# Edges ranked in 80 half-target buckets, one 314-column count matmul per chunk

## The reference

```python
for r in range(weight.shape[0]):
    mask = (edge_type == r).astype(x.dtype)
    sums = jax.ops.segment_sum(msgs * mask[:, None], dst, num_segments=n)
    cnt = jax.ops.segment_sum(mask, dst, num_segments=n)
    mean = sums / jnp.maximum(cnt, 1.0)[:, None]
    out = out + mean @ weight[r]
```

## Time and profile before

| what | us |
|---|---|
| median of three runs | 1880.85 |
| span of the profiled execution, first to last instruction | 1878.8 |
| what lies around the span, taken as median less span | 2.05 |
| edge tables, 38.2 to 142.0 | 103.8 |
| scatter, 142.0 to 242.3 | 100.3 |
| histogram, 242.3 to 429.0 | 186.7 |
| all that follows | 1449.8 |

### The profile page before, as it was taken

The page is one execution under the profiler, slowest core; times in us unless marked ns, Lnnn a source line. Parts: engine busy times, 40 slices in busy tenths (PEclk is TensorE's granted clock), DMA queues, the critical chain, the costliest instruction groups (busy, mean ns, idle before and its releaser), DMA issues.

```text
span 1878.8 us, 28666 instructions
## 1 busy us (share of the span) xinstructions
PE 1794.9 (96%) x9953; PEld 1477.4 (79%) x9953; DVE 1023.3 (54%) x2540; ACT 478.5 (25%) x1055; POOL 701.1 (37%) x609
## 2 busy tenths in 40 slices
PE   6999999999999999999999999954999999999999
PEld 4876689987777778787777887742899888878987
DVE  7888999997254543526354356786632224362311
ACT  3139956662010110101011145243100000111100
POOL 2110000003634435353534444200485552345862
PEclk9999999999999999999999999956999999999999
DMA  4532222224213121231313534110354351113322
GB/s 134 154 109 77 73 86 79 75 67 129 91 38 89 45 72 56 66 86 47 94 33 113 172 84 131 45 46 7 96 164 146 104 156 51 37 55 118 90 73 66
DMA packets 129282, 162.23 MB, mean 86 GB/s; under 512 B 14288, under 2 KB 75368, under 8 KB 128922
## 3 DMA queue, kind: packets, MB, share of 16 engines
q1 hardware_dynamic: 100848, 120.93, 21.5%
q10 hardware_dynamic: 22250, 23.53, 4.0%
q0 software_dynamic: 6080, 16.40, 2.9%
HBM read 135.51 MB, written 25.30 MB: 86 GB/s over the span
## 4 chain that ended last, share of the span: by engine, by line
PE 84%; DVE 6%; ACT 6%; issue 1%; DVEq 1%; DMA 1%; POOL 0%; ACTq 0%; SPq 0%
PE ps L367 22%; PE ps L368 22%; PE ps L369 21%; PE ps L1236 9%; PE ps L892 3%; ACT sc_col L838 2%; ACT sc_row L837 1%; PE ps L1201 1%; DVE w_lo L318 1%; PE ps L881 1%; PE ps L1156 1%; DMA nat<-in_x 1%; ACT w_hi L313 1%; PE ps L1183 1%; PE ps L1211 0%
## 5 line engine op out<-in xcount | busy, mean ns | idle before, releaser
L367 PE MATMUL ps<-w_hi,xt_hi 128*125 128x512 f32 x1320 | 539.0, 408 | 9.1 <-DVE xt_lo L549 3.5
L256 POOL TENSOR_TENSOR w_hi<-w_stage,zero 128x512 fp32r<-128x512 f32 x256 | 276.8, 1081 | 684.4 <-PE ps L369 670.0
L368 PE MATMUL ps<-w_lo,xt_hi 128*125 128x512 f32 x1320 | 523.0, 396 | 0.0
L369 PE MATMUL ps<-w_hi,xt_lo 128*125 128x512 f32 x1320 | 521.5, 395 | 0.0
L259 POOL TENSOR_TENSOR w_lo<-w_stage,w_hi 128x512 fp32r<-128x512 f32 x256 | 346.2, 1352 | 20.1
L367 PEld LDWEIGHTS ps<-w_hi,xt_hi 128*125 128x125 f32 x1320 | 246.6, 187 | 67.1 <-DVE xt_lo L549 4.3
L369 PEld LDWEIGHTS ps<-w_hi,xt_lo 128*125 128x125 f32 x1320 | 246.0, 186 | 63.3
L368 PEld LDWEIGHTS ps<-w_lo,xt_hi 128*125 128x125 f32 x1320 | 246.3, 187 | 53.5
L367 PE MATMUL ps<-xt_hi,w_hi 128*128 128x314 f32 x736 | 250.5, 340 | 1.3 <-DVE ring L2430 0.6
L369 PE MATMUL ps<-xt_hi,w_lo 128*128 128x314 f32 x736 | 225.9, 307 | 0.0
L368 PE MATMUL ps<-xt_lo,w_hi 128*128 128x314 f32 x736 | 225.7, 307 | 0.0
(11 more groups left out here) (392 smaller groups left out, 2390.2 us busy)
## 6 DMA issues: line engine op xcount, KB each, us to landing
w_stage<-in_stream SPq DMA_DIRECT2D x374, 256.0 KB, 2.7
pre<-ring POOLq DMA_DIRECT2D x30, 250.0 KB, 3.8
a_qt<-pre_t SPq DMA_DIRECT2D x18, 312.5 KB, 3.8
a_qt<-pre_t ACTq DMA_DIRECT2D x14, 312.5 KB
pre_t<-ring_t POOLq DMA_DIRECT2D x12, 312.5 KB, 2.8
pre_t<-ring_t ACTq DMA_DIRECT2D x12, 312.5 KB
a_vx<-pre SPq DMA_DIRECT2D x9, 312.5 KB
nat<-pre SPq DMA_DIRECT2D x2, 1250.0 KB
```

Source lines behind the costliest of these rows:

```text
L256: POOL.tensor_tensor(w_hi[:, q, :], w_stage[:, q % NST, :], zero[:].to_broadcast([128, 512]), ALU.add).then_inc(S("hi_done"), 1)
L367: PE.matmul(dst, l_hi, r_hi, start=first, stop=False)
L368: PE.matmul(dst, l_hi, r_lo, start=False, stop=False)
L369: return PE.matmul(dst, l_lo, r_hi, start=False, stop=last)
```

## The change

The buckets become 80 (`NKEY`): each block is halved by target, below 314 and from 314 on. A chunk of 128 edges is the unit; there are still 240, taken in 120 pairs.

- Edge tables: the 80 keys are 28 rows of up to three fields; each field is 8 bits of one number, so one running sum over 28x166 elements counts all. `key_hot` has 28 rows, `key_weight` is `key_hot` times 1, 2^8 or 2^16, `ranks` picks each edge's sum out of `scan`, `rank_fields` its field. The offset comes from 80 `tensor_scalar` operations (`key_start`), added up by halves. `edge_tables` puts fourteen small operations on GpSimd, ahead of its ring stores, which move down in its program unchanged.
- Histogram: `hot_col` has 314 columns; `hot_row` is made for four chunks at once, with a `tensor_tensor`; one matmul of 314 columns per chunk; ScalarE copies the two banks of a pair at once; VectorE adds 314 columns per chunk. A word of `gpack` holds three numbers of 7 bits.

```diff
-NGROUP = (EDGES + NBUCKET * (GROUP - 1)) // GROUP
-NCHUNK = 2 * NGROUP
+SPLIT = 314
+NKEY = 2 * NBUCKET
+FIELDS, NROW = 3, 28
+CHUNK = 128
+NCHUNK = (EDGES + NKEY * (CHUNK - 1)) // CHUNK
+NPAIR = NCHUNK // 2
...
+    def edge_tables(mk):
...
+        wait(POOL, mk)
+        POOL.tensor_scalar(wide, first, 2.0 ** 8 - 1.0, 1.0, ALU.mult, ALU.add)
...
+        POOL.tensor_copy(e_weight[:, 0:EC], wide)
+        POOL.drain().then_inc(S("e_more"), 1)
...
+        POOL.tensor_tensor(e_row1[:, 0:EC], e_row1[:, 0:EC], e_tile[:], ALU.add)
+        POOL.drain().then_inc(S("e_more"), 1)
...
+        DVE.tensor_tensor(key_hot[:], e_row[:].unsqueeze(1).to_broadcast([P, NROW, EW]),
+                          iota16[0:P, 0:NROW].unsqueeze(2).to_broadcast([P, NROW, EW]), ALU.is_equal)
+        split_low_dve(8, 11)
+        DVE.drain()
+        DVE.wait_ge(S("e_more"), 1)
+        DVE.tensor_tensor(key_weight[:], key_hot[:], e_weight[:].unsqueeze(1).to_broadcast([P, NROW, EW]), ALU.mult)
         evacuate(0)
         split_low_dve(11, 16)
         DVE.drain()
-        kh = key_hot[:].rearrange("p b c -> p (b c)")
-        DVE.tensor_tensor_scan(scan[:].rearrange("p b c -> p (b c)"), kh, kh, 0.0, ALU.add, ALU.max)
+        kw = key_weight[:].rearrange("p b c -> p (b c)")
+        DVE.tensor_tensor_scan(scan[:].rearrange("p b c -> p (b c)"), kw, kw, 0.0, ALU.add, ALU.max)
...
+    def ranks():
+
+        DVE.tensor_tensor(scan[:], scan[:], key_hot[:], ALU.mult)
+        DVE.drain()
+        n = NROW
+        while n % 2 == 0:
+            n //= 2
+            DVE.tensor_tensor(scan[:, 0:n], scan[:, 0:n], scan[:, n:2 * n], ALU.add)
+            DVE.drain()
+        DVE.tensor_reduce(e_rank[:], scan[:, 0:n].rearrange("p b c -> p c b"), AX.X, ALU.add)
...
     def positions(evacuate):
 
-        DVE.tensor_tensor(scan[:], scan[:], b_off[:].unsqueeze(2).to_broadcast([P, NBUCKET, EC]), ALU.add)
-        split_low_dve(24, 27)
-        DVE.drain()
-        DVE.tensor_tensor(scan[:], scan[:], key_hot[:], ALU.mult)
+        for b in range(NKEY):
+            DVE.tensor_scalar(key_start[:, b, :], e_key16[:], float(b), b_off[:, b:b + 1], ALU.is_equal, ALU.mult)
+            if b == NKEY // 2:
+                split_low_dve(24, 27)
         split_low_dve(27, 31)
+        evacuate(2)
...
+    def hist_hot(c):
+
+        if c % 4 == 0:
+            if c >= 8:
+                DVE.wait_ge(S("hi_pe"), c - 4)
+            DVE.tensor_tensor(hot_row[c // 4 % 2][:], iota1_by4[:],
+                              slot_row[:, c:c + 4].unsqueeze(1).to_broadcast([128, 128, 4]), ALU.is_equal)
+        if c >= 8:
+            DVE.wait_ge(S("hi_pe"), c - 7)
+        DVE.tensor_scalar(hot_col[c % 8][:], iota1_16[:, 0:SPLIT], slot_col[:, bass.ds(c, 1)], None,
+                          ALU.is_equal).then_inc(S("hi_dve"), 1)
+
+    def hist_copy(g):
+
+        b = pair_bank(g)
+        ALE.wait_ge(S("hi_pe"), 2 * g + 2)
+        if g >= 4:
+            ALE.wait_ge(S("hi_add"), 2 * g - 6)
+        ALE.activation(counts[g % 4][:], ps[0:P, b:b + 2, 0:SPLIT], ACT.Copy).then_inc(S("hi_main"), 1)
+
+    def hist_add(c, packed):
+
+        bucket = (packed >> (7 * (c % 3))) & 127
+        start = nc.s_assert_within((bucket >> 1) * NB + (bucket & 1) * SPLIT, 0, (NBUCKET - 1) * NB + SPLIT, ...)
+        DVE.wait_ge(S("hi_main"), c // 2 + 1)
+        if c:
+            DVE.wait_ge(S("hi_add"), c)
+        o = adj[:, bass.ds(start, SPLIT)]
+        DVE.tensor_tensor(o, o, counts[c // 2 % 4][:, c % 2, :], ALU.add).then_inc(S("hi_add"), 1)
+
+    def hist_pe(g):
+
+        if g >= 2:
+            PE.wait_ge(S("hi_main"), g - 1)
+        if g == 1:
+            PE.wait_ge(S("bank_free"), (SC0 + SC_GROUPS + 1) * T)
         for j in range(2):
...
+            c = 2 * g + j
+            PE.wait_ge(S("hi_dve"), c + 1)
+            PE.matmul(ps[0:P, pair_bank(g) + j, 0:SPLIT], hot_row[c // 4 % 2][:, 0:P, c % 4], hot_col[c % 8][:],
+                      start=True, stop=True).then_inc(S("hi_pe"), 1)
...
         mk = bucket_counts(evacuate)
         split_low_dve(16, 21)
+        ranks()
         dense(1)
         mk = bucket_sums(mk)
         evacuate(1)
         split_low_dve(21, 24)
-        mk = group_buckets(mk)
+        rank_fields()
+        mk = chunk_buckets(mk)
...
         for h in range(HI_GROUPS):
             for n in range(per):
...
+                for c in (2 * (h * per + n), 2 * (h * per + n) + 1):
+                    if c + LEAD_HOT < NCHUNK:
+                        hist_hot(c + LEAD_HOT)
+                    if c % 2 == 0 and chunk_at(h, n):
+                        split_dve(chunk_at(h, n))
+                    if c % 3 == 0:
+                        packed = DVE.value_load(gpack[0:1, c // 3:c // 3 + 1], min_val=0, max_val=2 ** 21 - 1)
+                    hist_add(c, packed)
```

More of the change, by code:

```diff
@@ L682, in build @@
     assert r_hot + sc_per * 1248 <= R_NAT + T * D * 4
[L683 to L688, removed]
+    slot_col = tmp("slot_col", [128, NCHUNK], F32, 1)
+    slot_row = tmp("slot_row", [128, NCHUNK], F16, 1)
+    hot_col = [tmp(f"hot_col{i}", [128, SPLIT], F16, 1) for i in range(8)]
+    hot_row = [tmp(f"hot_row{i}", [128, 128, 4], F16, 1) for i in range(2)]
+    zero16 = tmp("zero16", [P, 2 * NCHUNK], F16, 1)
+    iota1_by4 = at("iota1_by4", [128, 128, 4], F16, r_hot + sc_per * 1248)
+    assert r_hot + sc_per * 1248 + 1024 <= R_NAT + T * D * 4
+    counts = [at(f"counts{i}", [P, 2, SPLIT], I16, R_NAT + i * 1280) for i in range(4)]
     slot_ps = ps[:, 5, 0:2 * NCHUNK]
@@ L713, in bucket_counts @@
             DVE.drain()
-        DVE.tensor_scalar(e_row1[:, 0:EC], e_tile[:], -float(P), 1.0, ALU.mult, ALU.add)
         DVE.tensor_scalar(e_key[:], ed_typ[:], float(T), None, ALU.mult)
         DVE.drain()
-        DVE.tensor_tensor(e_row1[:, 0:EC], e_row1[:, 0:EC], ed_src[:], ALU.add)
         DVE.tensor_tensor(e_key[:], e_key[:], e_tile[:], ALU.add)
         DVE.drain()
[L721 to L726, removed]
+        DVE.scalar_tensor_tensor(e_key[:], e_key[:], 2.0, e_half[:], ALU.mult, ALU.add)
+        DVE.drain()
+        row, first = e_row[:, 0:EC], e_first[:, 0:EC]
+        DVE.tensor_scalar(first, e_key[:], float(NROW), None, ALU.is_ge)
+        DVE.tensor_scalar(e_second[:], e_key[:], float(2 * NROW), None, ALU.is_ge)
+        edge_tables(sig(DVE.drain(), "dve_step"))
+        DVE.scalar_tensor_tensor(row, first, -float(NROW), e_key[:], ALU.mult, ALU.add)
+        DVE.drain()
+        DVE.scalar_tensor_tensor(row, e_second[:], -float(NROW), row, ALU.mult, ALU.add)
+        DVE.drain()
+        DVE.tensor_tensor(key_hot[:], e_row[:].unsqueeze(1).to_broadcast([P, NROW, EW]),
+                          iota16[0:P, 0:NROW].unsqueeze(2).to_broadcast([P, NROW, EW]), ALU.is_equal)
+        split_low_dve(8, 11)
+        DVE.drain()
+        DVE.wait_ge(S("e_more"), 1)
+        DVE.tensor_tensor(key_weight[:], key_hot[:], e_weight[:].unsqueeze(1).to_broadcast([P, NROW, EW]), ALU.mult)
         evacuate(0)
@@ L811, in packed_buckets @@
         gflat = gcol[:].rearrange("o g j -> o (g j)")
-        DVE.tensor_scalar(gflat, ps[0:1, 6, 0:NGROUP], -1.0, None, ALU.add)
+        DVE.tensor_scalar(gflat, ps[0:1, 6, 0:NCHUNK], -1.0, None, ALU.add)
         DVE.drain()
@@ L860, in hist_copy @@
[L860 to L872, removed]
-        DVE.wait_ge(S("hi_add"), 4 + g)
-        o = adj[:, bass.ds(bucket * NB, NB)]
-        DVE.tensor_tensor(o, o, counts[gm][:], ALU.add).then_inc(S("hi_add"), 1)
@@ L877, in hist_pe_rest @@
[L877 to L893 removed]
+    LEAD_HOT = 4
@@ L975, in beside, with idle @@
                 DVE.wait_ge(S("sc_pe"), sc_per + EC + 1)
-                DVE.tensor_copy(slot[:, :, 0:NCHUNK], slot_ps.rearrange("p (a c) -> p a c", a=2))
+                DVE.tensor_copy(slot_col[:], slot_ps[:, 0:NCHUNK])
+                DVE.tensor_copy(slot_row[:], slot_ps[:, NCHUNK:2 * NCHUNK])
                 DVE.drain()
-                for n in range(2):
-                    hist_dve_hot(n, n)
+                for c in range(LEAD_HOT):
+                    hist_hot(c)
             evacuate(i + SC0)
-        ALE.sem_inc(S("hi_rest"), 2)
-        ALE.sem_inc(S("hi_main"), 2)
         HI0 = SC0 + SC_GROUPS
         assert HI0 + HI_GROUPS == G_PRE0
-        per = NGROUP // HI_GROUPS
-        assert per * HI_GROUPS == NGROUP and per * 4 == KT * T * 3
+        per = NPAIR // HI_GROUPS
+        assert per * HI_GROUPS == NPAIR and per * 4 == KT * T * 3
+        def idle(h, s_):
+            return s_ in (1, 2) or s_ > 2 and s_ % 4 == 3 and 3 < s_ < 36 if h == 0 else s_ % (4 if h < HI_GROUPS - 1 else 8) == (
+                3 if h < HI_GROUPS - 1 else 7)
         def hist_of(h, s_):
-            gap = 4 if h < HI_GROUPS - 1 else 8
-            n = s_ - s_ // gap
-            return n if s_ % gap != gap - 1 and n < per else None
+            n = sum(not idle(h, i) for i in range(s_))
+            return n if not idle(h, s_) and n < per else None
         def first_step(h, k):
@@ L1006, in between @@
```

(4 more changed lines are left out.)

239 lines of the change are left out of this document (131 added, 108 removed).

## The result

The changed kernel takes 1966.09 us (median of 4 runs, 1965.78 to 1967.89) against 1880.68 us before (4 runs, 1878.45 to 1880.96) on the same chip: a ratio of 1.0459, 95% interval 1.0444 to 1.0474. It is slower by 85 us; 69 were forecast, and 1966 lies in the range given.

What follows compares the result with a forecast made beforehand. TensorE bounds the edge tables, TensorE and VectorE together the histogram. Span 1878.8 + 13.7 (tables) + 56 (histogram) - 0.5 = 1948.0, with 2.05 around it 1950 us; the forecast's range is 1918 to 1990.

Steps and rivals of the forecast that it cites:

- Bound: Histogram: TensorE and VectorE both at their limit, 185.4 and 179.8 of 186.7 us, so a change must relieve both.
- the change's engine work: Histogram: VectorE 0.52 against 0.65 us per chunk, 31 us less; TensorE also 31 us less.
- The loop that closes: Histogram: each add waits for the previous one, then its address is computed; period 0.96 us, first to last add 238, +56.
- Loads: Histogram: a packed word's load takes 0.64 us, of which 0.37 sticks out beside the add, 0.12 per chunk.
- Splits: Histogram: 32 splits cost 0.6 us each, mostly into the gap: 0.25 each, 8 us.
- one longer fused operation, against a short one: Histogram, add's address: the fused operation grows, 0.03 us more, within 0.51 us from release to add.
- The upper bound of the period: Histogram: five single operations, a fused one like the load's 0.19 and an add of 0.48 give 1.25 us, 308 in all.
- The first rival, the address ready in time: Histogram: address computed before the waits or covered by the queue; stage 155 or 144 us, kernel 1863; chance 14%.
- The clock: Rival, histogram: TensorE's stops drop its clock to 1.2 GHz all through, 25 us more, 1975; chance 9%.
- The edge tables: Edge tables: VectorE's added work makes evacuate(1) 8.8 us later, evacuate(2) 4.9 more; the scatter starts 13.7 later.
- TensorE's stop ahead of dense group 2: Edge tables: TensorE, without slack, stands still there for as long as evacuate(1) is late, 8.8 us.
- GpSimd's part: Edge tables: its fourteen operations of 165 elements are hidden; without that cover the tables would cost about 5 us.

Runs made afterwards that it cites:

- fixed_place: Changed kernel with each chunk's counts added at a place fixed in advance, no word loaded, no address computed, result incomplete: 1855.23 us, ratio 0.9864 to the kernel before.
- before_fixed: Kernel before the change with counts of group g added at block g modulo 40, no word loaded or address computed, result incomplete: 1876.04 us, ratio 0.9981.
- early: Changed kernel with the start of the block computed into one of two registers before the add's waits: 1943.8 us, ratio 1.0336 to the kernel before.
- bare: Changed kernel with its packed words loaded without stated bounds: 1941.81 us, ratio 1.0333 to the kernel before.
- stride628: Changed kernel with count matrix blocks 628 columns apart instead of 626, so the address is one product: 1910.06 us, ratio 1.0159 to the kernel before.
- ranks_late: Changed kernel with ranks() placed behind evacuate(1) instead of ahead of it: 1967.64 us, ratio 1.0472 to the kernel before.
- best_tables: Changed kernel with early address, 628 stride, unbounded loads, four buckets a word, ranks split around evacuate(1), evacuate(2) inside the key_start loop: 1872.08 us, ratio 0.9957 to before.

## Why the prediction was right, and what its sum missed

- **Bound.** Right. Two engines were full in the histogram, and the sum of the change's engine work was right within 3 us: -31 forecast, -33.5 by fixed_place, -30 against before_fixed.
- **The loop that closes.** Right as a mechanism. From first to last add 238 were forecast and 259 came. By terms: a plain distance of 0.33 + 0.51 = 0.84 was taken, and 0.953 measured: 239 x 0.113 = +27. Loads: 29 forecast; the 79 distances with a load, the 20 with a split as well included, are together 103.5 us, 28 over 79 plain ones. Splits: 8 forecast; the other 11 distances with a split are together 3 over plain ones. So the term mis-sized is the step "one longer fused operation, against a short one", given 0.03 more. It had the number of operations right, 4.67 per chunk, but took 3.67 of them as single ones of 45 ns. The rows of after have 2.67 single and 2 fused, of 76 and 129 ns in the chain above. That is 0.03 for the first and 0.04 over the 0.085 allowed for the second, and the remaining 0.04 is put down to handing over and to waits for ScalarE's counts (23 us in all), which no run took apart. The upper bound of the period, 1.25, is 1.32 by its own terms (0.35 + 3 x 0.08 + 0.13 + 0.48 + 0.12), which the forecast's range didn't use.
- **The first rival, the address ready in time.** It had the price right, 144 to 155 for the engines' work, where 147.9 came with no address. Early, which makes the address as early as that rival wanted, shows why it fell: with the arithmetic ahead of the waits the plain distance is still 0.77 us, since the sequencer's own work for a chunk doesn't fit beside an add and a table. The Trainium skill, "Advanced Engine Details and Errata", Engine Queue Depths, gives the queue a depth of 8; no run here shows such a queue covering the register work of this loop: in early VectorE still sat idle 54 us in all for "issue" ahead of its adds.
- **The clock.** The forecast gave it 9%, and expected stretches at half clock rather than half clock all through. Two neighbouring windows in after, the second at 1.2 GHz:

```profile
285.00:292.00 7.00, 4.56 (x25) 3.58 (x24) 4.27 (x16) 2.87 (x5) 0.55 (x1) 1.00 0.31 87
293.00:296.40 3.40, 3.35 (x13) 3.29 (x14) 2.46 (x8) 0.69 (x1) 0.00 (x0) 0.51 0.06 17
297.00:304.00 7.00, 4.89 (x29) 3.88 (x28) 4.60 (x16) 3.61 (x7) 0.57 (x1) 1.00 0.02 6
```

  TensorE was busy 65% ahead of it, and at half clock 99%. There are nine such stretches of 3.4 us among the 257, mean clock 0.94 instead of the 0.5 of the rival. What they cost wasn't measured by itself. In the loop of adds they would show as waits for counts: 23 us in all, of which 19 stayed in bare at a clock of 0.98, and 4 in stride628 at 1.00. How much of these is the clock stays open. The Trainium skill, "TensorE: Matmul & The Clock Gate", Part 1, says that activity releases the clock; the last two rows agree.
- **The edge tables.** evacuate(1) was forecast 8.8 later and came 8.8 later, with running sum (9.84 for 9.8), multiply (4.99 for 5.0) and reduce (2.24 for 2.4) as taken. evacuate(2), and with it the scatter, was forecast 13.7 later; it came 8.0 later, and the first add 8.6. Of the 5.7, 4.4 are key_start, 7.20 / 41 = 0.175 us each, not 0.23 (80 x 0.23 is 18.4; the sum had 18.8). The extra 0.06 for a second operation, read from fp16 tables at two widths, didn't apply. It was nearer to the lower bound of 0.16. That TensorE's stop ahead of dense group 2 is what carries over to the scatter was part of the step; ranks_late, where the stop moved and nothing was gained, speaks against that, and for VectorE's own work as what sets the scatter's start, apart from the 3 us of best_tables.
- **GpSimd's part** was hidden, as forecast: its tables end at 58.8, and the ring stores behind them start at 59.45.
- **Sum.** Tables -5 and histogram +21 against the forecast make +16, the distance from 1950 to 1966. That the two misses have opposite signs is luck; the histogram by itself was 21 out of 77.

## What to carry to other kernels

Before an operation with a computed address is made smaller and more frequent, count the sequencer's instructions per step and add their rows; where each step waits for the last one, that sum and the step's own duration are the period, and an "idle, issue" on an engine that looks free is the sign of it. Then make the address cheap (equal strides, so that it is one product; no bounds on the load; more numbers to a word) and move it ahead of the wait: the cheaper product alone gave 56 us and the earlier address alone 22. Each alone left the kernel slower than before, all together made it slightly faster. Work of one engine between two releases of another's buffers can be split instead of moved whole: ranks_late moved the stop, best_tables cut it from 7.3 to 1.5 us, and 3.0 us of waiting came back at the scatter.

## What the runs showed of the hardware

- Register operations of VectorE's sequencer: single ones 45 ns, fused ones 46 ns (early's add line), 57 (stride628), 76 and 129 (the changed kernel), by what they combine, with 0.03 us between them. A load with bounds has a fused operation of 205 ns and a check of 23 ns more than one without.
- Weights read from a table with four chunks side by side loaded slower than from a table of their own chunk; whether the distance between elements is the reason wasn't tried by itself. The rows over the histogram of before and of after:

```profile
L892 PEld LDWEIGHTS ps<-hot_col,hot_row 128*125 128x125 f16 x236 | 27.8, 136 | 11.8 <-DVE hot_row L857 6.4
```

```profile
L961 PEld LDWEIGHTS ps<-hot_col,hot_row 128*125 128x125 f16 x238 | 45.8, 194 | 100.4 <-DVE hot_col L930 64.4 <-ACT counts L939 29.4 <-issue 6.1
```

  136 ns became 194, and it isn't the clock: fixed_place has 192 at a clock of 1.00. It hides beside matmuls here: fixed_place, with the same loads, has TensorE busy 147 us where 155 were forecast.
- One of GpSimd's operations on 165 elements took 4.64 us, its neighbours 0.6 to 0.7, while VectorE made `key_hot` (5.00 us from 44.73); another, 2.40 us from 52.59, ran beside `key_weight` (2.58 us from 52.23). Whether that is what slowed it wasn't tried.

```profile
44.51 0.66 POOL L703 TENSOR_SCALAR e_pos<-e_second 125x165 f32<-125x165 f32 x1
45.49 4.64 POOL L705 TENSOR_TENSOR e_wide<-e_wide,e_pos 125x165 f32<-125x165 f32 x1 [0.33 <-issue]
```
